# Self attention: two heads stacked on 128 partitions, their products in the two row halves of TensorE, and the row maxima applied by a product of one row

## The reference

```python
q = (src @ Wq + bq).reshape(B, T, N_HEAD, HEAD_DIM)      # 4 x 512 x 16 x 16
k = (src @ Wk + bk).reshape(B, T, N_HEAD, HEAD_DIM)
v = (src @ Wv + bv).reshape(B, T, N_HEAD, HEAD_DIM)
scores = jnp.einsum('bqhd,bkhd->bhqk', q, k) * scale
probs = jax.nn.softmax(scores, axis=-1)
attn = jnp.einsum('bhqk,bkhd->bqhd', probs, v).reshape(B, T, D_MODEL)
```

## Time and profile before

| | us |
|---|---|
| median of 3 runs (1731.36 to 1739.45) | 1737.66 |
| the profiled execution | 1756.76 |
| its span | 1755.0 |
| first score product of the self attention | at 422.53 |
| last division of its results begins | at 661.84 |
| PE, DVE, ACT busy in the whole span | 1557.9, 1085.6, 837.7 |

### The profile page before, as it was taken

The page is one execution under the profiler, slowest core; times in us unless marked ns, Lnnn a source line. Parts: engine busy times, 40 slices in busy tenths (PEclk is TensorE's granted clock), DMA queues, the critical chain, the costliest instruction groups (busy, mean ns, idle before and its releaser), DMA issues. The chain is left out here.

```text
span 1755.0 us, 24380 instructions
## 1 busy us (share of the span) xinstructions
PE 1557.9 (89%) x8332; PEld 1035.9 (59%) x8332; DVE 1085.6 (62%) x2751; ACT 837.7 (48%) x1337; POOL 479.0 (27%) x261
## 2 busy tenths in 40 slices
PE   7899999989999996599956998889898998999992
PEld 5566666566544444399934555555663556677771
DVE  5799999655677858346566888888733530122223
ACT  3688888633566671322227777777332121211110
POOL 0201100012000000301117999999022143111111
PEclk9999999989799998899978999999979999999996
DMA  7454422025343314567656888997060012144434
GB/s 246 162 160 145 150 85 66 21 75 177 80 113 106 93 37 150 201 206 252 231 207 233 301 278 294 299 299 267 1 217 0 1 51 76 56 155 157 149 111 159
DMA packets 139208, 266.20 MB, mean 152 GB/s; under 512 B 25296, under 2 KB 69840, under 8 KB 129744
## 3 DMA queue, kind: packets, MB, share of 16 engines
q1 hardware_dynamic: 132896, 249.55, 43.5%
q0 software_dynamic: 5136, 14.06, 2.2%
q10 hardware_dynamic: 1056, 1.05, 0.2%
HBM read 206.98 MB, written 57.60 MB: 151 GB/s over the span
## 5 line engine op out<-in xcount | busy, mean ns | idle before, releaser
L683 DVE CUSTOM_DVE_ANT_0 X<-pS,M 128x512 f32<-128x512 f32 x512 | 340.5, 689 | 57.0 <-POOL M L610 40.6
L633 PE MATMUL pT<-ident,X 128*128 128x128 f32 x2048 | 305.5, 272 | 1.9 <-ACT PT L723 1.9
L624 PE MATMUL pS<-k,q 65*128 65x512 f32 (+1 forms) x512 | 254.2, 496 | 53.2 <-DVE mx L683 38.0
L610 POOL TENSOR_TENSOR M<-C,M 128x2048 f32<-128x2048 f32 x63 | 286.1, 4591 | 8.8 <-DMA M<-in_fside_Bx16xSxS 8.3
L633 PEld LDWEIGHTS pT<-ident,X 128*128 128x128 f32 x2048 | 254.2, 140 | 41.4 <-issue 4.2
L484 PE MATMUL pO<-PT,V 128*17 128x512 f32 x1536 | 203.1, 604 | 1.0 <-ACT OT L912 1.0
L624 PEld LDWEIGHTS pS<-k,q 65*128 65x128 f32 (+1 forms) x512 | 98.0, 191 | 172.8 <-DVE mx L683 107.1
L883 DVE TENSOR_REDUCE nm<-pS 128x1 fp32r<-128x512 f32 x256 | 164.9, 686 | 46.8 <-PE pS L825 37.9
L713 ACT ACTIVATE X<-X,nm 128x512 f32<-128x512 f32 x256 | 164.0, 712 | 28.7 <-DVE nm L689 28.7
L713 ACT ACTIVATE X<-X,mx 128x512 f32<-128x512 f32 x256 | 165.1, 716 | 3.9 <-DVE mx L683 3.6
L698 DVE COPY PT<-pT 128x1024 f32<-128x1024 f32 x128 | 156.1, 1220 | 6.4 <-PE pT L633 6.4
(11 more groups left out here) (309 smaller groups left out, 2160.8 us busy)
## 6 DMA issues: line engine op xcount, KB each, us to landing
M<-in_fside_Bx16xSxS SPq DMA_DIRECT2D x64, 1024.0 KB, 7.4
w<-in_L_ffn_ew SPq DMA_DIRECT2D x48, 512.0 KB, 5.8
w<-in_L_ffn_W SPq DMA_DIRECT2D x23, 1024.0 KB, 8.2
q<-q_stacks SPq DMA_DIRECT2D x192, 64.0 KB, 3.8
k<-k_stacks SPq DMA_DIRECT2D x128, 64.0 KB, 3.0
xs<-top_in SPq DMA_DIRECT2D x51, 128.5 KB, 2.1
k_stacks<-hi SPq DMA_DIRECT2D x24, 256.0 KB, 2.0
q_stacks<-hi SPq DMA_DIRECT2D x24, 256.0 KB, 2.0
```

The costliest lines, as they stand in the source:

```text
L610: eng.tensor_tensor(M[:, slot], C[:, b % 2], M[:, slot], ALU.subtract).then_inc(s_m, 1)
L624: eng.matmul(pS[:, qt % 2, :], of, by, start=True, stop=True).then_inc(s_s, 1)
L633: ins = eng.transpose(pT[:, kt, qt * P:(qt + 1) * P], X[:, t % 3, qt, kt * P:(kt + 1) * P], self.ident[:])
L683: eng.tensor_tensor_reduce(X[:, i % 3, qt, :], pS[:, qt % 2, :], M[:, slot, qt, :], 2.0 if not per_group else 1.0, HIGHEST if not per_grou ...
```

## The change

A pair of heads takes the place of a head as the unit of the loop (PAIRS = 32). The stacks of two heads stand one above the other on 128 partitions: head j in rows 64j to 64j + 63, so `q` and `k` of a pair have one slot of 128 x 512 instead of 64 x 2 x 512. The stacks in DRAM are new tensors with another order of rows (`q_rows`, `k_rows`), loaded by 8 DMAs for a pair (`load_piece`) instead of 6.

One step (four to a pair) has two score products, one on rows 0 to 63 and one on rows 64 to 127, into two banks of `pS`; two turned products in the same way, into two banks of `pT`; and two products of one row each, which add -1 (`neg`) times the maxima (`sh`, at partitions 0 and 64) to the same banks of `pT`. In the built program the score and turned products have tiles of 64 x 128 of PE at row positions 0 and 64, the one-row products tiles of 32 x 128 at row positions 0 and 64, the transposes 128 x 128, and the products with the values 128 x 32.

The maxima of a head go from `nT` into `sh` by one DMA within SBUF (two for a pair), not through DRAM. LAG is 2 pairs (4 heads) where it was 6 heads. A `weigh` stands behind every second step. During the first two pairs that are turned, a product of two identities stands in each step, and ACT loads the table for the exponential before the loop. GpSimd's memsets of the padding rows go.

```diff
-        LAG = 6
+        LAG = 2
...
-            pT = self.ps("pT", [P, ST, 512], ctx)
+            pT = self.ps("pT", [P, 2, 2, 512], ctx)
...
                         eng.wait_ge(s_nc, pair + 1)
-                        eng.dma_start(shift[pair], nT[:, pair % 2, :]).then_inc(s_out[pair % 2], 16)
-                        if pair + 3 < NBH // 2:
-                            load(pair + 3)
-                        eng.wait_ge(s_out[pair % 2], 16 * (pair // 2 + 1))
-                        eng.dma_start(q[SHIFT:SHIFT + 1, pair % RING].rearrange("o h s -> o (h s)").bitcast(F32),
-                                      shift[pair:pair + 1].rearrange("o a c -> o (a c)")).then_inc(s_sh[pair % RING], 16)
+                        for j in range(2):
+                            eng.dma_start(sh[j * AUX:j * AUX + 1, pair % RING].bitcast(F32),
+                                          nT[j * ST:(j + 1) * ST, pair % 2, :]).then_inc(s_sh[pair % RING], 16)
+                        ahead = pair + 3
+                        if ahead < PAIRS:
+                            need(eng, s_t, ST * (ahead - RING + 1))
+                            for piece in range(6):
+                                if piece < 2:
+                                    self.load_piece(eng, QS, q, ahead % RING, ahead, piece, 0, s_qk[ahead % RING])
+                                self.load_piece(eng, KS, k, ahead % RING, ahead, piece, 1, s_qk[ahead % RING])
...
+                    def scores(pair, qt):
+                        slot = pair % RING
+                        if qt == 0:
+                            eng.wait_ge(s_qk[slot], 128 * (pair // RING + 1))
+                        for j in range(2):
+                            rows = slice(j * AUX, (j + 1) * AUX)
+                            empty("scores", pair, 2 * qt + j)
+                            eng.matmul(bank("scores", pair, 2 * qt + j), q[rows, slot, qt * P:(qt + 1) * P], k[rows, slot, :],
+                                       start=True, stop=True).then_inc(s_s, 1)
+
+                    def turned(pair, kt):
...
+                        if kt == 0:
+                            moved(eng, pair)
+                        need(eng, s_e, ST * pair + kt - 1)
+                        for j in range(2):
+                            rows = slice(j * AUX, (j + 1) * AUX)
+                            eng.matmul(pT[:, kt % 2, j, :], k[rows, slot, kt * P:(kt + 1) * P], q[rows, slot, :], start=True, stop=False)
+                        for j in range(2):
+                            row = slice(j * AUX, j * AUX + 1)
+                            ins = eng.matmul(pT[:, kt % 2, j, :], neg[row, :], sh[row, slot, :], start=False, stop=True)
+                        ins.then_inc(s_t, 1)
...
+                            if 0 <= pair < 2:
+                                eng.matmul(pO[:, 0:P], self.ident[:], self.ident[:], start=True, stop=True)
```

More of the change, by code:

```diff
@@ L34 @@
 NG = NBH // GROUP
-SHIFT = AUX + 32
+PAIRS = NBH // 2
 BEHIND = 6
@@ L274, in project @@
             aq, ak, s_ahead = ahead
-            pieces = [(pair, third) for pair in range(len(s_ahead)) for third in range(3)]
+            load_piece = self.load_third if first else self.load_piece
+            pieces = [[(pair, piece) for pair in range(len(s_ahead)) for piece in range(count)] for count in ((3, 3) if first else (2, 6))]
             spread = half - 2
@@ L840, in back @@
-                    def back(g):
-                        eng.wait_ge(s_oc, g)
-                        empty("values", g, 0)
-                        for qt in range(ST):
-                            ins = eng.transpose(bank("values", g, 0)[:, qt * P:(qt + 1) * P], OT[:, qt * P:(qt + 1) * P], self.ident[:])
-                        ins.then_inc(s_b, 1)
+                        if qt == 0:
[5 more added lines that the diff above has]
+                                       start=True, stop=True).then_inc(s_s, 1)
@@ new lines, in _ @@
+                            if c == 0 and 0 <= i - 1 < PAIRS:
+                                eng.wait_ge(s_x, 2 * ST * i)
+                                empty("maxima", i - 1, 0)
+                                eng.transpose(bank("maxima", i - 1, 0)[0:2 * ST, 0:P], nm[:, (i - 1) % 2, :].bitcast(F32), self.ident[:])\
+                                   .then_inc(s_nt, 1)
+                            if 0 <= pair < PAIRS:
+                                turned(pair, c)
+                            if 0 <= pair < 2:
+                                eng.matmul(pO[:, 0:P], self.ident[:], self.ident[:], start=True, stop=True)
@@ new lines, in _ @@
+                            g, odd = divmod(i - LAG - 4, 2)
+                            if c == 1 and odd == 0 and 0 <= g < NG:
+                                eng.wait_ge(s_oc, g + 1)
+                                empty("values", g, 0)
+                                for qt in range(ST):
+                                    ins = eng.transpose(bank("values", g, 0)[:, qt * P:(qt + 1) * P], OT[:, qt * P:(qt + 1) * P], self.ident[:])
+                                ins.then_inc(s_b, 1)
+                            g, kt = divmod(2 * (i - LAG - 2) + c // 2, ST)
@@ L888, in _ @@
                 @block.scalar
                 def _(eng):
+                    eng.activation(warm[:], self.ident[:, 0:2], ACT.Exp)
                     for i in range(LAST):
-                        h = i - LAG
-                        g, j = divmod(h, GROUP)
-                        if i % 2 == 0 and 0 <= i // 2 - 1 < NBH // 2:
-                            pair = i // 2 - 1
-                            eng.wait_ge(s_nt, pair + 1)
-                            need(eng, s_out[pair % 2], 16 * (pair // 2))
-                            eng.copy(nT[:, pair % 2, :], bank("maxima", pair, 0)[0:2 * ST, 0:P]).then_inc(s_nc, 1)
@@ L910, in _ @@
+                        g, odd = divmod(i - LAG - 3, 2)
+                        if odd == 0 and 0 <= g < NG:
                             eng.wait_ge(s_o, g + 1)
```

189 lines of the change are left out of this document (87 added, 102 removed).

## The result

| | before | after |
|---|---|---|
| median, us | 1738.56 (4 runs) | 1893.3 (4 runs, 1873.38 to 1897.33) |
| ratio to before | | 1.0869, 95% interval 1.0828 to 1.0910 |
| span of the profiled execution | 1755.0 | 1888.2 |
| first score product at | 422.53 | 442.31 |
| stage, to the end of the last division | 239.7 | 368.9 |

The changed kernel is slower by 155 us, where 36 were forecast. In the two profiled executions the stage takes 129.2 us more, it starts 19.8 us later, and the unchanged rest happens to be 15.7 us shorter. For the experiments the stage is taken to the first product of the next one, which is 0.3 to 0.7 us later than here; for before that is 240.4 us.

The account below looks back on a forecast made before the run. PE was taken to bound, DVE close behind. Two pairs: 14.1 us of work plus 2.5 of waits, 8.35 a pair; with start and end the stage takes 275.7 against 239.7, +36: 1774 us, range 1735 to 1832.

Parts of the forecast that it names:

- the paragraph on the clock: Start of the stage: identity products may save 8 us or emptyings lower the clock elsewhere; +36 us left unchanged.
- rival 3: Steady part: a third runs at 1.2 GHz, a pair there takes 12.8 us, +40 us, 1814; chance 0.14.
- 0.4 us later start: SP in `project`: 18 key loads instead of 9, three after the last store instead of two, delay the start 0.4 us.
- rival 2: PE's couples: row halves don't overlap, each couple costs up to 0.23 us more, +62 on top, 1836; chance 0.09.
- Rival 1: PE's steps: changes of tile cost nothing, weights are loaded ahead, 6.35 us a pair, -22 us, 1716; chance 0.13.
- The step: PE's three couples with weights and two emptyings: 1.11 us, replacing four products at 0.93 us.
- A pair without division: Pair with the waits of its second and fourth steps, without the division or the values' way back: about 7.4 us.
- (a): Second step of a pair: its second score product waits 0.4 us for a bank, twice per two pairs.
- (c): Fourth step of the other pairs, those without the division: a wait of 0.2 us.
- The wait for the division: Fourth step of every second pair: first score product waits 1.5 us for DVE's division, after the third step's reductions.
- The move within SBUF at nothing: Maxima moved by two DMAs per pair: up to 2.9 us, hidden in a pair's 8 us, costed at nothing.
- The shorter lag: LAG from six heads to four: 11.8 us instead of 16.6 at the start, 19.1 instead of 21.0 at the end.

Follow-up runs that it names:

- e2: Changed kernel with its one-row products made 64-row products, 63 rows zero: 1798.11 us, ratio 1.0253 to before.
- e7: Kernel before with the maxima moved by one DMA within SBUF instead of through DRAM: 1753.79 us, ratio 1.0021.
- e10: Kernel before with a small 32-row product, in another tile, ahead of each turned product: 2114.37 us, ratio 1.2188.
- e1: Changed kernel with the old order of rows in DRAM and loads that fit it: 1885.12 us, ratio 1.0767 to before.
- e5: e2 with DVE's division ahead of the third step's reductions instead of behind them: 1784.42 us, ratio 1.0217 to before.
- e8: e7 with LAG of 4 heads, identity products in the 16 steps turned without values, and the early table load: 1742.17 us, ratio 0.9965 to before.
- e3: Changed kernel without the one-row products, so the maxima are not subtracted: 1798.64 us, ratio 1.0270 to before.
- e9: Kernel before with a small 128-row product, in its neighbours' tile, ahead of each turned product: 1776.07 us, ratio 1.0238.
- e4: Changed kernel with one more 128 x 128 identity product in each step, ahead of the turned products: 1951.63 and 1992.91 us.

## Why the prediction was wrong

**What failed.** The forecast's direction held and its size did not: +155 us for +36, outside the range of 1735 to 1832. The step that failed is the paragraph on the clock: "I leave +36 as it is". It puts the cost of the lower clock at nothing, and keeps a fall to 1.2 GHz for a third of the steady part as rival 3, at a chance of 0.14 and 1814 us. What rival 3 describes is what happened, for some 255 of the 369 us of the stage and not for a third. The stage was forecast at 276 us and took 369, so 93 us more. No long pair of the changed kernel ran wholly at the full clock, so its stage at that clock is an estimate: at the lower level pairs took 11.8 and 13.8 us by turns, 12.8 in the mean, so 255 us are 20 pairs; at the forecast 8.35 us each these would take 88 us less, 281 in all. e2 shows it measured, without the changes of tile: 106 us less at the full clock.

The sum over the whole program is then 36 forecast, 93 of the clock and 19 of the start (next), 148 of the 155 us. A further 8 us lie in the base: the 239.7 us of before, from which the forecast subtracts, contain the fall of the clock, and the executions behind the median for the most part probably do not (e7's profile has 232.2).

The argument against the rival was the wrong one. "The values keep it up from 468 us on" took one kind of product for the cause; in the kernel before, a set of values with its two changes of tile came once in 3.4 us, and in the changed kernel there are two changes in each step of 1.1 us besides. The prediction saw this, as "PE standing empty for 0.2 of 1.1 us", and gave it too little weight. e10 shows it alone: +382 us for a product that costs 44 in the right tile. The earlier trace rows already showed that the clock can be low while PE is recorded as 100% busy, so a busy PE was no argument that it would stay up.

**Second, the start.** "0.4 us later start" was 19.8 us. The prediction counted SP's issues at the 0.42 us of the steady part and counted 18 loads, but it took the stores to be the same stores. Written to the new order, a store takes SP 0.57 us and more instead of 0.32, and small loads between them 0.45 to 1.0; SP then can't keep pace with the projections, ACT waits for the buffers of the stores (20 us in 8 waits, none in the kernel before), and the stage waits for the last issue. With the old order (e1) 12.4 of the 19.8 us come back, and 7.4 are left with the loads. This was a term set to nothing whose cover, SP's spare time in the projections, was never checked.

**What held, step by step.**

- The halves overlap: the two turned products of a couple start within 0.01 us of each other in 114 of 128 couples of the trace, and rival 2 falls. Rival 1 (changes of tile cost nothing) falls too.
- The step: 1.11 us predicted, 1.09 measured. At the lower clock 1.9 predicted, 1.87 measured. A pair at that clock, predicted 12.8, takes 11.8 and 13.8 by turns, 12.8 in the mean.
- A pair without division: about 7.4 by the forecast's terms (half of 14.1 and its waits (a) and (c), less the way back), 7.36 measured, in e1 at the full clock (470.76 to 478.12).
- The wait for the division, 1.5 us: 20.0 us in 13 waits in e2, and 1.2 us a time come back in e5.
- Without changes between 64 and 32 rows a pair was said to take 7.9: e2 takes (7.0 + 8.8) / 2 = 7.9.
- The move within SBUF at nothing: e7. In the changed kernel PE waited once for the maxima, 0.5 us, and once for a load, 0.4.
- The 8 us that the clock cost at the start of the stage before: e7's stage, without the fall, is 8.2 us shorter.
- The shorter lag was credited with 6.7 us at start and end (4.8 and 1.9). e8 against e7 shows 3, with the identity products' cost in it.

The Trainium skill, "TensorEngine Tiling (Array Packing)", Key Properties, was cited for the drain, and by that rule the time of a step came out right. What the drain does to the clock is in no row of the prediction, and the page does not speak of it.

**What stays open.** Whether the chip answers to the change of tile itself or only to the spells in which PE stands empty was not separated. e3, whose clock swings without changes between 64 and 32 rows, speaks for the latter, but its recorded busy share is only 3 points below that of e2, whose clock held. Nor was a one-row product without a change of tile tried.

Nor do the runs say why the order of rows makes an issue longer; they show only its length (0.32 and 0.57 us) and the later start. The Trainium skill, "DMA: Bandwidth & Descriptors", section "Why a DMA increments its semaphore by 16 and not by 1", says that a DMA is spread over the largest number of engines, up to 16, that divides the slowest dimension of both patterns. By that rule a store of 128 rows in one stride would go over 16 engines and one of 8 heads by 16 rows over 8. No run here shows the engines of a single DMA, so this is a candidate and no finding.

## What to carry to other kernels

Price a change of TensorE's tile not by its 0.1 us alone but by what it may do to the clock: where tiles of different rows alternate within a microsecond, try to give every product the same number of rows, with zero rows if need be, as the 63 zero rows here gained some 105 us. Put a filler into the tile of its neighbours (e9, e8) and not between two changes (e4, e10), and read the granted clock of the stage and not the busy share. Before an access pattern in DRAM is changed for convenience of the reader, look at how long the issuing queue takes for one transfer of it, and whether that queue has time to spare where it is issued.

## What the runs showed of the hardware

- Two products on rows 0 to 63 and 64 to 127 take the time of one: a couple of 512 columns starts 0.33 us after another of the same tile whose weights were not loaded ahead, as a single product did in the earlier trace rows (0.34).
- Tiles of 32 and 128 rows in alternation kept the clock at 0.50 for 587 us on end (441 to 1028), with PE recorded as busy for 30.00 of 30 us (e10). The record of busy time does not show it.
- One store of 256 KB took its queue 0.32 us in one order of rows and 0.57 us in the other, and up to 3.6 us in the change, close behind other issues.
